# Output projection, its normalisations and the residual of a cross-attention done inside the attention's loop over batches

## The reference, cut to what matters

```python
q, k, v = proj(hs, Wq, bq), proj(at, Wk, bk), proj(at, Wv, bv)      # 16 heads of 32
scores = clip(q k / sqrt(32), -50, 50), masked keys at -50
ctx = softmax(scores) v
delta = rs * (ctx @ Wo.T + bo)                                      # rs: one number
delta = (delta - mean) / sqrt(var + 1e-5) * ln_gamma + ln_beta
x = x + delta
n = layernorm(x)
x = x + (silu(n Wg.T) * (n Wu.T)) Wd.T                              # Wg, Wu, Wd from integers
```

## Time and profile before

| | |
|---|---|
| runs of the kernel before | 569.55 us median of three, 568.96 to 572.02 |
| the profiled execution | 575.04 us, span 573.3 us from the first to the last instruction |
| mean granted clock of TensorE | 0.943 of full speed |
| PE busy | 484.9 us (85%) |
| DVE busy | 323.9 us (56%) |
| ACT busy | 237.4 us (41%) |
| POOL busy | 81.8 us (14%) |
| second attention | 331.0 to 414.7 us from the span's start |
| output projection | 414.7 to 461.5 us |
| feed-forward up to the down product | 461.5 to 534.3 us |

### The profile page before, as it was taken

The page is one execution under the profiler, slowest core; times in us unless marked ns, Lnnn a source line. Parts: engine busy times, 40 slices in busy tenths (PEclk is TensorE's granted clock), DMA queues, the critical chain, the costliest instruction groups (busy, mean ns, idle before and its releaser), DMA issues. The chain is left out here.

```text
span 573.3 us, 10040 instructions
## 1 busy us (share of the span) xinstructions
PE 484.9 (85%) x3946; PEld 363.5 (63%) x3954; DVE 323.9 (56%) x529; ACT 237.4 (41%) x351; POOL 81.8 (14%) x68
## 2 busy tenths in 40 slices
PE   3599999997496969999949987978757679999997
PEld 2487878786384546666628766766645535555896
DVE  4834356512375674666644235786779986565311
ACT  3334443433137435556645275856411415212000
POOL 3100040001230400000020001111274550000000
PEclk9899999998788989999996989999969889999999
DMA  8976557932437012111026589776034050000011
GB/s 261 389 268 244 181 179 245 319 130 61 133 119 266 19 44 90 33 46 47 23 85 275 110 168 360 298 277 220 3 115 189 0 202 0 0 1 1 16 63 50
DMA packets 30364, 79.29 MB, mean 138 GB/s; under 512 B 5105, under 2 KB 18417, under 8 KB 27249
## 3 DMA queue, kind: packets, MB, share of 16 engines
q1 hardware_dynamic: 30320, 78.69, 40.5%
q10 hardware_dynamic: 2, 0.01, 0.0%
HBM read 58.76 MB, written 14.42 MB: 128 GB/s over the span
## 5 line engine op out<-in xcount | busy, mean ns | idle before, releaser
L167 PE MATMUL psum<-wv_p,kv_p 128*128 128x512 f32 x288 | 80.4, 431 | 8.9 <-DVE wv_p L623 5.5
L165 PE MATMUL psum<-kv_p,wk_p 128*128 128x384 f32 x384 | 76.6, 352 | 11.9 <-PEq L668 7.3
L165 PEld LDWEIGHTS psum<-kv_p,wk_p 128*128 128x128 f32 x384 | 69.6, 196 | 14.6 <-issue 10.2
L167 PEld LDWEIGHTS psum<-wv_p,kv_p 128*128 128x128 f32 x288 | 56.8, 201 | 25.7 <-issue 13.5
L1341 ACT ACTIVATE e<-psum,mask_bias 128x448 f32<-128x448 f32 x96 | 53.6, 636 | 22.0 <-PE psum L1362 22.0
L1376 PE MATMUL psum<-e,vst 128*32 128x112 f32 x768 | 38.9, 269 | 8.4 <-issue 4.3
L187 DVE SCALAR_TENSOR_TENSOR khl<-psum,bqk,khl 128x384 f16<-128x384 f32 x32 | 19.7, 616 | 42.9 <-ACT khl L177 42.7
L1397 DVE TENSOR_SCALAR e<-e 128x1344 f32<-128x1344 f32 x32 | 29.2, 925 | 25.9 <-ACT e L1341 25.9
L1743 PE MATMUL psum<-xt,wg_b 128*128 128x448 f16 x176 | 38.3, 362 | 5.0 <-DVEq L1788 5.0
L181 ACT ACTIVATE vsp<-psum 128x512 f32<-128x512 f32 x24 | 14.3, 597 | 63.7 <-PE psum L167 63.7
L315 POOL TENSOR_SCALAR w_stage<-w_stage,w_stat 128x2816 f32<-128x2816 f32 x6 | 18.7, 3125 | 132.3 <-DVE w_stat L310 132.3
(11 more groups left out here) (176 smaller groups left out, 826.0 us busy)
## 6 DMA issues: line engine op xcount, KB each, us to landing
kst<-k_scratch SPq DMA_DIRECT2D x8, 1536.0 KB, 9.7
kv_raw<-in_ctx_feat SPq DMA_DIRECT2D x12, 768.0 KB, 5.7
w_stage<-in_w SPq DMA_DIRECT2D x6, 1408.0 KB, 7.2
cn<-in_ctx_tok SPq DMA_DIRECT2D x8, 768.0 KB, 6.4
k_scratch<-khl SPq DMA_DIRECT2D x128, 48.0 KB, 1.7
v_scratch<-vsp SPq DMA_DIRECT2D x24, 256.0 KB, 2.6
vst<-v_scratch SPq DMA_DIRECT2D x8, 768.0 KB, 5.8
w_int<-in_wg SPq DMA_DIRECT2D x2, 1408.0 KB, 7.4
```

What stands on the lines that cost most here:

```text
L165: mm = pe.matmul(psum[:, kv_bank(p), 0:TP], wk_p[:, u, k, n * P:(n + 1) * P], src[:, v, k, :], **ends)
L167: mm = pe.matmul(psum[:, kv_bank(p), :], src[:, u, k, n * P:(n + 1) * P], wv_p[:, v, k, :], **ends)
```

## The change

The block of the output projection is gone. Batch b of the attention now carries, beside its own work, `context_high`, `context_low` and the product (`project`) of tile b-2, and the variance, delta, residual, statistics and the turn of the normalised x of tile b-3. Tile 6's product and the rest of tiles 5 and 6 come in the first rounds of the feed-forward block, as do all seven turns of the new x (`x3_turn`). To make room in PSUM, values and sums have one bank each. Each engine's list is rewritten; statistics are per tile, not per group. The integers of the weights are loaded and converted in chunks of 512 columns (22 for Wg and Wu during the attention, 11 for Wd in the feed-forward part). SyncE loads Wo before the second part of the queries. Much of SBUF is laid out anew.

The attention block, and the functions that it calls:

```diff
+        def integers_load(sp, n):
+            after(sp, wi_ready, n - 1)
+            cols = slice(n % JC * D, (n % JC + 1) * D)
+            sp.dma_start(w_int[n % 2][:], (wg, wu, wd)[n // JC][:, cols]).then_inc(wi_loaded[n % 2], 16)
+        def integers(pool, n):
+            cols = slice(n % JC * D, (n % JC + 1) * D)
             out_w = (wg_b[:].rearrange("p k n -> p (k n)"), wu_b[:].rearrange("p k n -> p (k n)"),
...
+                     wd_r[:].rearrange("p j n -> p (j n)"))[n // JC]
+            if n == JC:
+                pool.wait_ge(q_stacked[1], STACK)
+            pool.wait_ge(wi_loaded[n % 2], 16 * (n // 2 + 1))
+            pool.tensor_scalar(out_w[:, cols], w_int[n % 2][:], -ZERO_POINT, 1.0, ALU.add, ALU.mult).then_inc(wi_ready, 1)
...
+        def value_bias(pool, b):
+            pool.wait_ge(ctxt_scaled, b + 1)
+            pool.tensor_tensor(ctxt[:, :, b * S:(b + 1) * S], ctxt[:, :, b * S:(b + 1) * S],
+                               bqk[:, 2, :].rearrange("p (k o) -> p k o", o=1).to_broadcast([P, KC, S]), ALU.add).then_inc(ctxt_ready, 1)
+        def delta_inverse(pool, t):
+            pool.wait_ge(y_var, t + 1)
+            pool.tensor_tensor(estat[:, 1, t], estat[:, 0, t], neg_half[:, 0:1], ALU.pow).then_inc(y_rstd, 1)
+        def x3_inverse(pool, t):
+            pool.wait_ge(x3_mv, t + 1)
+            pool.tensor_scalar(rstd[:, t], ln_mv[:, t, 1:2], LN_EPS, 1.0, ALU.add, ALU.mult).then_inc(x3_var, 1)
+            pool.wait_ge(x3_var, t + 1)
+            pool.tensor_tensor(rstd[:, t], rstd[:, t], neg_half[:, 0:1], ALU.pow).then_inc(x3_rstd, 1)
+        def context_high(act, t):
+            act.wait_ge(ctxt_ready, t + 2)
+            after(act, o_sum, t - 1)
+            act.activation(ctxt_p[t % 2][:, 0], ctxt[:, :, t * P:(t + 1) * P], ACT.Copy).then_inc(ctxt_hi, 1)
...
+        def project(pe, t):
+            pe.wait_ge(ctxt_lo, t + 1)
+            pe.wait_ge(wo_lo, 1)
+            after(pe, y_ready, t)
             for k in range(KC):
-                mm = pe.transpose(psum[:, E_X + t % 2, k * P:(k + 1) * P], xres[:, t, k * P:(k + 1) * P], ident[:])
-            mm.then_inc(x3_turned, 1)
+                for u, v in PARTS:
+                    mm = pe.matmul(psum[:, E_O, :], ctxt_p[t % 2][:, u, k, :], wo_p[:, v, k, :],
+                                   start=(k, u, v) == (0, 0, 0), stop=(k, u, v) == (KC - 1, *PARTS[-1]))
+            mm.then_inc(o_sum, 1)
+        def normalized_turn(pe, t):
             pe.wait_ge(f_xn, t + 1)
-            after(pe, xt_lo, t - 1)
+            after(pe, xt_lo, t)
             for k in range(KC):
-                mm = pe.transpose(psum[:, E_N + t % 2, k * P:(k + 1) * P], xn_e[:, t % 2, k * P:(k + 1) * P], ident[:])
+                mm = pe.transpose(psum[:, E_N, k * P:(k + 1) * P], xn_e[t % 2][:, k * P:(k + 1) * P], ident[:])
             mm.then_inc(f_turned, 1)
...
+        def context_low(dve, t):
+            dve.wait_ge(ctxt_hi, t + 1)
+            dve.tensor_tensor(ctxt_p[t % 2][:, 1], ctxt[:, :, t * P:(t + 1) * P], ctxt_p[t % 2][:, 0].bitcast(F32),
+                              ALU.subtract).then_inc(ctxt_lo, 1)
+        def delta_variance(dve, t):
+            dve.wait_ge(o_sum, t + 1)
+            dve.tensor_tensor(y[t % 2][:], psum[:, E_O, :], rows3[:, 0, :], ALU.add).then_inc(y_ready, 1)
+            dve.wait_ge(y_ready, t + 1)
+            dve.bn_stats(ln_stat[:, t, :], y[t % 2][:]).then_inc(y_stats, 1)
+            dve.wait_ge(y_stats, t + 1)
+            dve.bn_aggr(ln_mv[:, t, :], ln_stat[:, t, :]).then_inc(y_mv, 1)
+            dve.wait_ge(y_mv, t + 1)
+            dve.tensor_scalar(estat[:, 0, t], ln_mv[:, t, 1:2], rs[:, 1:2], LN_EPS, ALU.mult, ALU.add).then_inc(y_var, 1)
+            dve.scalar_tensor_tensor(y[t % 2][:], y[t % 2][:], ln_mv[:, t, 0:1], rows3[:, 1, :], ALU.subtract,
+                                     ALU.mult).then_inc(y_norm, 1)
+        def x3_statistics(dve, t):
+            dve.wait_ge(y_rstd, t + 1)
+            dve.tensor_scalar(estat[:, 2, t], estat[:, 1, t], rs[:, 0:1], None, ALU.mult).then_inc(y_scale, 1)
+            dve.wait_ge(y_scale, t + 1)
             dve.wait_ge(y_norm, t + 1)
             dve.wait_ge(beta_added, t + 1)
-            dve.scalar_tensor_tensor(xres[:, t, :], y[:, t, :], estat[:, 2, t], xres[:, t, :], ALU.mult,
+            dve.scalar_tensor_tensor(xres[:, t, :], y[t % 2][:], estat[:, 2, t], xres[:, t, :], ALU.mult,
                                      ALU.add).then_inc(x3_ready, 1)
...
+        def x3_shift(dve, t):
+            dve.wait_ge(x3_rstd, t + 1)
+            dve.scalar_tensor_tensor(estat[:, 3, t], ln_mv[:, t, 0:1], -1.0, rstd[:, t], ALU.mult, ALU.mult).then_inc(f_shift, 1)
```

SyncE, POOL and ScalarE in it:

```diff
+            def chunks(lo, hi):
+                for n in range(lo, min(hi, GU_CHUNKS)):
+                    integers_load(sp, n)
+            sp.dma_start(wk_raw[:], wo).then_inc(proj_loaded[0], 16)
+            queries_stack(sp, 1)
+            chunks(0, 2)
+            for b in range(B - 2):
+                sp.wait_ge(s_sum, TC * G * (b + 1))
+                keys_fetch(sp, b + 2, b % 2)
+                chunks(4 * b + 2, 4 * b + 4)
+                sp.wait_ge(pv_sum, G * (b + 1))
+                values_fetch(sp, b + 2, b % 2)
+                chunks(4 * b + 4, 4 * b + 6)
...
+            def chunks(lo, hi):
+                for n in range(lo, min(hi, GU_CHUNKS)):
+                    integers(pool, n)
+            for b in range(B):
+                chunks(4 * b, 4 * b + 2)
+                if b:
+                    value_bias(pool, b - 1)
+                if b >= 3:
+                    delta_inverse(pool, b - 3)
+                if b < TILES:
+                    residual(b)
+                if b >= 3:
+                    x3_inverse(pool, b - 3)
+                chunks(4 * b + 2, 4 * b + 4)
...
+            exps(0)
+            exps(1)
+            for b in range(B):
+                for g in range(G):
+                    m = G * b + g + 2
+                    if m < G * B:
+                        exps(m)
+                    if (b, g) == (1, 0):
+                        act.wait_ge(proj_loaded[0], 32)
+                        act.activation(wo_p[:, 0], wk_raw[:], ACT.Copy).then_inc(wo_hi, 1)
+                    if g == 1 and b >= 4:
+                        turned_high(act, b - 4)
+                    if g == 2 and b >= 2:
+                        context_high(act, b - 2)
+                    if g == 3 and b >= 3:
+                        x3_normalized(act, b - 3)
```

TensorE and VectorE in it:

```diff
+                pe.wait_ge(e_ready, G * b + g + 1)
+                if g == 0:
+                    pe.wait_ge(vst_loaded[b % 2], 16 * (b // 2 + 1))
+                    after(pe, ctxt_scaled, b)
...
+            scores(0)
+            scores(1)
+            for b in range(B):
+                for g in range(G):
+                    m = G * b + g + 2
+                    if m < G * B:
+                        scores(m)
+                    values(b, g)
+                if b >= 2:
+                    project(pe, b - 2)
+                if b >= 3:
+                    normalized_turn(pe, b - 3)
...
+            def normalize(b):
+                dve.wait_ge(pv_sum, G * (b + 1))
+                after(dve, ctxt_scaled, b)
+                dve.reciprocal(rz[:], psum[:, D_Z, 0:G * S].rearrange("p (g s) -> p g s", g=G)).then_inc(z_inv, 1)
+                dve.wait_ge(z_inv, b + 1)
+                dve.tensor_tensor(ctxt[:, :, b * S:(b + 1) * S], psum[:, D_U, 0:G * S].rearrange("p (g s) -> p g s", g=G),
+                                  rz[:], ALU.mult).then_inc(ctxt_scaled, 1)
...
+            clip(0)
+            clip(1)
+            for b in range(B):
+                if b:
+                    normalize(b - 1)
+                clip(G * b + 2)
+                if b >= 3:
+                    delta_variance(dve, b - 3)
+                clip(G * b + 3)
+                if b == 1:
+                    dve.wait_ge(wo_hi, 1)
+                    dve.tensor_tensor(wo_p[:, 1], wk_raw[:], wo_p[:, 0].bitcast(F32), ALU.subtract).then_inc(wo_lo, 1)
+                if b >= 4:
+                    turned_low(dve, b - 4)
+                if b >= 3:
+                    x3_statistics(dve, b - 3)
+                if b + 1 < B:
+                    clip(G * b + 4)
+                if b >= 3:
+                    x3_shift(dve, b - 3)
+                if b + 1 < B:
+                    clip(G * b + 5)
+                if b >= 2:
+                    context_low(dve, b - 2)
+            normalize(B - 1)
```

The feed-forward block:

```diff
-            group_inverse(pool, 2)
-            integers(pool, 4)
-            integers(pool, 5)
+            value_bias(pool, B - 1)
+            delta_inverse(pool, 5)
+            integers(pool, GU_CHUNKS)
+            x3_inverse(pool, 5)
+            integers(pool, GU_CHUNKS + 1)
+            delta_inverse(pool, 6)
+            integers(pool, GU_CHUNKS + 2)
+            x3_inverse(pool, 6)
+            for n in range(GU_CHUNKS + 3, 3 * JC):
```

(58 more changed lines are left out.)

384 lines of the change are left out of this document (94 added, 290 removed).

## The result

The changed kernel takes 580.63 us (median of 4 runs, 576.77 to 580.75) against 570.78 (568.96 to 572.31) of the kernel before: ratio 1.0156, interval 1.0109 to 1.0204. A second series gave 579.8 against 572.78, ratio 1.0127 (1.0093 to 1.0162). It is slower, by 7 to 10 us, where +5.3 was forecast and 575.0 given. The measured time is inside the range, 561 to 584.

What follows compares the result with a forecast made beforehand. It took the old middle stage as bound by no full engine and the feed-forward by TensorE, with VectorE's order setting the new attention's period. Terms +3.8 and +1.5 gave +5.3 on the 569.55 us median: 575, range 561 to 584.

Steps and rivals of the forecast that it cites:

- five signs named: Periods 16 to 18 us; TensorE idle over 4 us, then half clock; slow scalar operation; feed-forward at 465; its first part 74.
- +9.6: Batches 0 to 2 of the attention: us lost before the added work begins, putting normalize(2) at 375.0.
- +4.8, +2.1 and +2.7: Batches 0 to 2: us for single-bank waits, for keys late behind weight loads, for value bias behind chunk conversions on POOL.
- +1.4 a batch: Batches 3 to 7: us added to each product because TensorE's clock falls after its idle gap; bounds 0 and 2.3.
- the clock stays up: Rival for the attention's products: no cold product, 8.4 us less, 566.5 us; chance 20%.
- Sum 16.2: Batches 3 to 7: VectorE's period in us before the clock term, bare 14.6 plus contention with POOL; bounds 14.6 and 17.5.
- The residual's +0.6: Batches 3 to 7: us a batch because POOL's residual add delays the small scalar operation that begins x3_statistics.
- Chunks and value bias (+0.3): Batches 3 to 7: us added to VectorE's period by POOL's chunk conversions and value bias.
- +3.8 and +1.5: Us by which the feed-forward begins later (465.3 against 461.5), and by which its first part grows (74.3 against 72.8).
- the same for the median: Final step: the +5.3 us found on the profiled execution (575.04) was applied unchanged to the median 569.55, giving 575.
- The bare cycle: Rival for the attention: VectorE's cycle without POOL contention, periods 14.6, start at 371, 558 us; chance 17%.
- the late fetches: Rival for the attention: keys land 2 us late in four batches, queued behind chunk loads waiting for POOL, 583 us; chance 13%.

Runs made afterwards that it cites:

- e1: Changed kernel with context_high and context_low right after the turns of high and low in batches 3 to 7, x's turn behind the first value group; 571.78 us, ratio 0.9984.
- e3: Changed kernel with 14 unused matmuls (8 in batch 7) filling TensorE's gap before the product in batches 3 to 7; 570.5 us, ratio 0.996 to the kernel before.
- e2: Changed kernel with two PSUM banks for values and sums in batches 0 to 2; 581.48 us, ratio 1.0168 to the kernel before.
- e8: Changed kernel with e2's banks, weight chunks loaded from batch 1 on and converted at batch ends from batch 2 on; 575.17 us, ratio 1.0044 to the kernel before.
- e6: Changed kernel with all of POOL's residual adds moved ahead of the first batch; 580.28 us, ratio 1.016 to the kernel before.
- e10: e9 with POOL's chunk conversions at the start of a batch instead of its end; 565.21 us, ratio 0.9878 to the kernel before.
- e7: e1 with two score groups instead of one ahead of the first value group in batches 3 to 7; 566.99 us, ratio 0.9918 to the kernel before.
- e9: e7 and e8 together, with context_high and context_low early from batch 2 on; 557.84 us, ratio 0.9716 to the kernel before.

## Why the prediction was right, and where not

**The mechanism** was as told: a ring over context_low, product, scores, exponentials and first clip, with VectorE in it. Of the five signs named, four are there in the main: periods of 16.8 in batches 4 to 6 (15.5 or 17.2 in batch 3, 15.4 in batch 7); waits of 3.9 to 4.7 us before the products (2.8 before the last), released by ctxt_p, with half the clock behind them; the feed-forward at 461.9 and 466.0; its first part 73.4 us. One is not: x3_statistics' small scalar operation takes 0.20, not over 0.5. That the ring is the cause and not only seen beside it was shown twice: e1, which takes context_low out of it, and e3, which makes one link shorter, give 8 and 9 us.

**Batches 0 to 2.** Forecast: normalize(2) at 375.0; it came at 374.7 and 376.3. The step "+9.6" was however built as a sum of three terms, +4.8, +2.1 and +2.7, each of its own. They are not additive. The bank wait is as large as said (3.97 and 4.71), but e2, without it, gains nothing, because the keys (3.86) and the value bias (4.08) end as late. e8, without the bank wait and without chunks ahead of keys and bias, takes batches 1+2 from 28.0 or 30.5 to 22.9, 5 to 8 us. The sum fitted; its division did not, so the fit is in part luck. It also left out the clock, which was 0.77 and 0.89 there. Which of chunk loads, conversions and the lower clock weighs more was not separated, nor what the chunks would do if moved alone.

**The clock.** +1.4 a batch was taken, 1.55 measured (16.80 to 15.25 in e3). The rival "the clock stays up" fell: every product behind a wait of about 4 us was slow. The first product, with a shorter wait, was warm in one profile and slow in the other. The Trainium skill (TensorE: Matmul & The Clock Gate, HAM oscillation) has every tile starting cold in such a loop. The trace agrees in that every product from the second tile on was slow, and not in how it starts: in batch 5 it started at 1.00 and the clock fell within it. So 12 matmuls took 4.5 to 4.6 us in most batches, where e6's at half rate throughout took 5.4.

**VectorE's contention** was over-sized: "Sum 16.2" was 15.25 measured warm (e3), so 0.65 over the bare 14.6 instead of 1.6. x3_inverse's wait is as said (0.71 at the shift). The residual's +0.6 is 0.6 in batch 3 but 0.2 in batches 4 to 6 (e6), and it falls on the full-width x3_add, not on the scalar operation that was named. The term rested on a row in which a scalar operation waited for an add; here the add began 0.9 us ahead of L1420 and the operation still took 0.20. Chunks and value bias (+0.3) cost nothing in batches 4 to 6: they run while VectorE has its reciprocal or waits for the scores, and batch 6, which has no chunks, has the same 16.8. With the bare path to the first clip of 5.65 (measured 5.61 to 5.64) the cycle came out at 17.6, measured 16.80: contention 0.95 too much, clock 0.15 too little. The sum for batches 3 to 7, 84.3, measured 81.7 and 82.9.

**The power operations** were rightly put at nothing for VectorE. The two-input operation L1414 ran beside L1357's for 0.58 us and took 0.74, as without it. L1414 had begun first (417.19 against 417.35), and it was POOL's operation that was long: 1.39 us, where the same kind on one column, L1363, took 0.55. The Trainium skill (GPSIMD Engine Reference, Key points) lets POOL contend with VectorE instructions of two SBUF inputs; for a power operation on one column no such cost shows. For conversions it does (e8: 0.68 to 1.08), and for the residual add (batch 3: 0.75 to 1.36).

**End of the attention:** from normalize(7) the forecast had 6.0 us, measured 5.5 and 6.8; the longer is a product wholly at half rate (5.49) and a turn likewise. **Feed-forward:** 74.3 forecast for its first part, 73.4 measured, +0.7 on before instead of +1.5; the end of the kernel took 0.7 more (39.7 us against 39.0), which I had at nothing. It is the down product itself, 36.38 us against this of before; why stays open.

```profile
534.31 35.69 PE psum L1766 x176
```

**The sum.** +3.8 and +1.5, measured +4.5 and +1.4 in the second profile: +5.9 against +5.3, on spans. The step that failed is "the same for the median". Before's profile lay 4.3 us over the median of the four runs (5.5 over the three known then), and those of the changed kernel 3.9 under and 1.1 over theirs. So +5.3 on the profile gives 580.3, where 580.9 came; from the median it gives 575.0, where 580.6 came. The kernel before spreads from 567.3 to 576.4 us over the runs of the experiments' four series, with medians of 570.3 to 574.0, so its profile was a long one. What makes it long or short stays open; no trace of a short one was read. Other steps were off in size and partly made up for one another: VectorE's contention, the division of the early batches, the down product.

**The rivals.** The bare cycle did not come (normalize(2) would have been at 371, periods 14.6), nor the late fetches in batches 3 to 7: the trace has no wait for keys there. The queue behind POOL's chunks did act, in the early batches (e2) and in e10, where the batch is short.

## What to carry to other kernels

When work of one stage is put into another, write down who waits for whom over one whole turn; what decides here is not any engine's load (in each batch VectorE had over 4 us free, and TensorE 4 us in one piece) but that the last instruction of one engine's turn releases the first of another's. Moving context_low, the transposes and a score group within the batch is worth 12 us here (e7); with the early batches mended as well (e9) the same idea is 16 us faster than the kernel before, not 7 to 10 slower. Parallel late arrivals are not added up: here removing one (e2) showed nothing while the others stood. And once a ring leaves TensorE idle for some us in one piece, count its next matmuls at the lower clock.
